# Two graph-attention layers on one core: TensorE's turns two units ahead, the first quad's features ahead of the second's root, and the last three units split in a half and two quarters

## What is computed

```
# first layer: softmax attention under the mask of adj
S = (x @ Wq) @ (x @ Wk).T
P = softmax(S + mask, axis=1)      # mask: lowest float where adj + eye is 0, highest where it is 2
x = layernorm(x + P @ (x @ Wv))
# second layer: additive attention
h = x @ W.T + b
e = leaky((h @ a1)[:, None] + (h @ a2)[None, :] + b_a)
attention = softmax(where(adj > 0, e, -9e15), axis=1)
x = layernorm(x + attention @ h)
```

## Time and profile before

| what | value |
|---|---|
| median of 3 runs | 253.81 us (253.43 to 254.62) |
| profiled execution, its own time | 255.0 us |
| its span, first to last instruction | 253.2 us |
| mean granted TensorE clock | 0.983 |
| PE busy | 236.2 us (93%) |
| DVE busy | 185.3 us (73%) |
| ACT busy | 154.4 us (61%) |
| POOL busy | 61.4 us (24%) |

### The profile page before, as it was taken

One profiled execution on the slowest core, in us unless ns is written; L12 is line 12 of the kernel. 1 busy time (PEld: TensorE's weight loads), 2 busy tenths in 40 slices (PEclk: granted clock), 3 DMA queues, 4 the chain that ended last, 5 costly groups with the idle time before them and its releaser, 6 DMA issues.

```text
span 253.2 us, 4017 instructions
## 1 busy us (share of the span) xinstructions
PE 236.2 (93%) x1523; PEld 133.3 (53%) x1523; DVE 185.3 (73%) x284; ACT 154.4 (61%) x182; POOL 61.4 (24%) x104
## 2 busy tenths in 40 slices
PE   5959999499999999999999999999999999999980
PEld 4947675245555555555555555555555555555450
DVE  1378787967777777779768776977777778797433
ACT  2468978989067999170489994610899982220032
POOL 3284688999200000003030000002300000032122
PEclk9999999679999999999999999999999999999998
DMA  6999999999999999999589999998499920010102
GB/s 187 365 386 389 383 387 383 387 387 386 385 388 383 380 384 387 387 386 385 64 237 305 332 403 392 387 387 298 114 299 339 397 99 3 1 41 3 41 3 88
DMA packets 40939, 71.76 MB, mean 283 GB/s; under 512 B 5843, under 2 KB 6100, under 8 KB 40916
## 3 DMA queue, kind: packets, MB, share of 16 engines
q1 hardware_dynamic: 40480, 71.33, 79.2%
q10 hardware_dynamic: 436, 0.13, 0.2%
HBM read 69.36 MB, written 2.10 MB: 282 GB/s over the span
## 4 chain that ended last, share of the span: by engine, by line
PE 86%; POOL 3%; ACT 3%; DMA 2%; DVE 2%; issue 2%; ACTq 1%; POOLq 0%; DVEq 0%
PE banks L1202 67%; PE banks L1158 10%; PE banks L1217 3%; PE banks L1095 3%; DMA brow<-in_L_gnn_b_W_dram 2%; ACT a L737 2%; PE banks L1110 1%; POOL rstd L597 1%; PE banks L1081 1%; DVE y L1036 0%; POOL f_parts L636 0%; POOL xhat_st L602 0%; POOL frstd L646 0%; POOL feat L629 0%; DVE e_sb L938 0%
## 5 line engine op out<-in xcount | busy, mean ns | idle before, releaser
L1202 PE MATMUL banks<-e_sb,f_parts 128*128 128x512 f16 x768 | 186.1, 391 | 1.5 <-DVE e_sb L938 1.1
L926 DVE SCALAR_TENSOR_TENSOR e_sb<-R,cr_word,banks 128x1024 f32<-128x1024 f32 x124 | 153.8, 1275 | 30.9 <-PE banks L1158 28.3
L737 ACT ACTIVATE a<-a_sb,code_bias 128x2048 fp8e4<-128x2048 int32 x64 | 124.3, 1997 | 2.8 <-DMA a_sb<-in_adj_dram 2.1
L1202 PEld LDWEIGHTS banks<-e_sb,f_parts 128*128 128x128 f16 x768 | 71.6, 97 | 86.8 <-issue 4.0
L646 POOL TENSOR_TENSOR frstd<-frv,minus_half 128x4 f32<-128x4 f32 x8 | 8.1, 1012 | 168.9 <-DVE frv L962 167.6
L1158 PE MATMUL banks<-ident,a 128*128 128x128 f16 x496 | 38.0, 220 | 3.6 <-ACT a L737 3.6
L1158 PEld LDWEIGHTS banks<-ident,a 128*128 128x128 f16 x496 | 32.8, 98 | 15.4 <-ACT a L737 3.9
L728 ACT COPY R<-banks 128x512 f32<-128x512 f32 x8 | 4.7, 587 | 35.9 <-PE banks L1110 35.9
L753 ACT ACTIVATE junk<-y 128x128 f32<-128x128 f32 x28 | 8.3, 298 | 26.8 <-DVE y L953 26.8
L944 DVE RECIPROCAL rden<-banks 128x4 f32<-128x4 f32 x7 | 1.3, 183 | 12.2 <-PE banks L1217 12.2
L1095 PEld LDWEIGHTS banks<-m0c_um,x_tr 128*128 128x128 f32 x64 | 9.6, 224 | 0.8
(11 more groups left out here) (113 smaller groups left out, 101.9 us busy)
## 6 DMA issues: line engine op xcount, KB each, us to landing
a_sb<-in_adj_dram SPq DMA_DIRECT2D x64, 1024.0 KB, 12.4
x_sb<-in_x_dram SPq DMA_DIRECT2D x8, 256.0 KB, 9.9
out_dram<-out_sb SPq DMA_DIRECT2D x8, 256.0 KB, 5.8
w_nat<-in_L_gnn_W_dram ACTq DMA_DIRECT2D x1, 64.0 KB, 3.2
wv<-in_L_gnn_Wv_dram ACTq DMA_DIRECT2D x1, 64.0 KB, 3.1
acol<-in_L_gnn_a_vec_dram SPq DMA_DIRECT2D x1, 1.0 KB, 3.0
bcol<-in_L_gnn_b_W_dram ACTq DMA_DIRECT2D x1, 0.5 KB, 4.5
ba<-in_L_gnn_b_a_dram ACTq DMA_DIRECT2D x1, 0.0 KB
```

The source lines that it names most:

```text
L737: nc.scalar.activation(a8[:, n % 2, Q * h:Q * (h + 1), k * PW:(k + 1) * PW], a_parts[:, m % SLOTS, :, :], ACT.Relu, bias=code_bias[:, :], ...
L926: nc.vector.scalar_tensor_tensor(out=e_sb[:, k % NE, :], in0=R[:, g % 2, :], scalar=cr_word[:, 0, 2 * t + b:2 * t + b + 1], in1=ps_code[s ...
L1202: ins = nc.tensor.matmul(ps_acc[g % 2][h][:, :], f[:, j, :], e_half[:, k % NE, cols, part], start=(j == 0 and n == 0), stop=(j == T - 1 an ...
```

## The change

It has three parts. **Middle:** the turns stay two units ahead, behind the sums, until slot 9 (`LATE = QUADS + 1`) instead of slot 4; slot 9 then makes up the third unit. **Start:** on SP the first piece of `adj` is loaded ahead of the second quad of `x`; on PE `weights(1)` and `layer0(0)` stand ahead of `x_turned(1)`, and four matmuls of `keep_busy` go; on ACT `codes(0)` stands ahead of `copy_xt(1)`; on DVE `words(0)` stands ahead of `divide(1, scores)`; on POOL the first half of quad 0's features stands ahead of `root(1)`. **End:** the second 512 rows of the last three units become two quarters of 256 rows; the last quarter is summed in a bank of its own (`ps_last`) and added by DVE to what earlier units left.

```diff
@@ sizes
-    FIRST = QUADS - 4
+    LATE = QUADS + 1
+    LAST = GW - 2 * P
+        ps_last = ps_row[:, 0:2 * P]
@@ SP
                 load_x(0)
...
+                load(0)
                 load_x(1)
-                load(0)
@@ POOL
                 root(0)
+                features(0, 0)
                 root(1)
-                features(0, 0)
                 features(0, 1)
@@ ACT
                 copy_xt(0)
-                copy_xt(1)
                 act.wait_ge(consts_ready, 12)
                 codes(0)
+                copy_xt(1)
                 exps(0)
                 exps(1)
...
+                act.wait_ge(half_done, 2)
+                nc.scalar.copy(acc_t[:, HW:GW], ps_acc[g % 2][1][:, :]).then_inc(acc_copied, 1)
                 squares(g, 0)
-                act.wait_ge(half_done, 2)
-                for k in range(2):
-                    cols = slice(k * HW // 2, (k + 1) * HW // 2)
-                    nc.scalar.copy(acc_t[:, HW:GW][:, cols], ps_acc[g % 2][1][:, cols]).then_inc(acc_copied, 1)
@@ DVE
                 divide(0, scores)
                 divide(0, inner)
+                words(0)
                 dve.wait_ge(rstd_ready, 2)
                 divide(1, scores)
-                words(0)
                 words(1)
                 half_edges(0, 0, 0)
...
+                    if k == 0:
+                        dve.wait_ge(half_done, 3)
+                        dve.wait_ge(acc_copied, 2 * G)
+                        nc.vector.tensor_tensor(acc_t[:, LAST:GW], ps_last[:, :], acc_t[:, LAST:GW],
+                                                ALU.add).then_inc(acc_copied, 1)
@@ PE, last_sums
-                    for s in units:
-                        for b in range(2):
-                            ins = products(s, b, 1)
-                        if s == S - HALVED:
-                            pe.wait_ge(acc_copied, 2 * G - 1)
-                            pe.wait_ge(y_ready, 2 * G - 2)
-                            projections(0, quad(0), range(Q)).then_inc(fin_mm, 1)
-                    ins.then_inc(half_done, 1)
+                    pe.wait_ge(r_ready, 2 * G)
                     for k in range(2):
-                        pe.wait_ge(acc_copied, 2 * G + k)
-                        projections(1, quad(4), range(2 * k, 2 * k + 2)).then_inc(fin_mm, 1)
+                        for s in units:
+                            if s == S - 1:
+                                if k == 0:
+                                    pe.wait_ge(acc_copied, 2 * G - 1)
+                                    pe.wait_ge(y_ready, 2 * G - 2)
+                                    projections(0, quad(0), range(Q)).then_inc(fin_mm, 1)
+                                else:
+                                    pe.wait_ge(acc_copied, 2 * G)
+                                    projections(1, quad(4), range(2)).then_inc(fin_mm, 1)
+                            for b in range(2):
+                                ins = products(s, b, (slice(HW, LAST), slice(LAST, GW))[k])
+                        ins.then_inc(half_done, 1)
+                    pe.wait_ge(acc_copied, 2 * G + 1)
+                    projections(1, quad(4), range(2, 4)).then_inc(fin_mm, 1)
@@ PE, start
                 weights(0)
+                weights(1)
+                layer0(0)
                 x_turned(1)
-                weights(1)
-                keep_busy(bank[0], 4)
-                layer0(0)
                 layer0(1)
@@ PE, slots
-                    if FIRST < slot < S - NA:
+                    if LATE < slot < S - NA:
                         turn(slot + NA)
                     if slot < S - HALVED:
                         sums(slot)
...
-                    if slot <= FIRST:
+                    if slot <= LATE:
                         turn(slot + 2)
-                    if slot == FIRST:
+                    if slot == LATE:
                         turn(slot + 3)
```

More of the change, by code:

```diff
@@ L1177, in half_sums @@
                         pe.wait_ge(p_half if h == 0 else p_ready, 2 * s + b + 1)
-                        ins = products(s, b, h)
+                        ins = products(s, b, halves[h])
                         if h == 1:
@@ L1193, in sums, with products @@
                         pe.wait_ge(p_ready, 2 * s + b + 1)
-                        products(s, b, 0)
-                        products(s, b, 1).then_inc(mm_done, 1)
-                def products(s, b, h):
+                        products(s, b, halves[0])
+                        products(s, b, halves[1]).then_inc(mm_done, 1)
+                def products(s, b, cols):
                     g, t = divmod(s, U)
                     k, j = 2 * s + b, 2 * t + b
-                    cols = slice(h * HW, (h + 1) * HW)
+                    h, first = divmod(cols.start, HW)
+                    dst, opened = ps_acc[g % 2][h][:, first:first + cols.stop - cols.start], j == 0
+                    if cols.start == LAST:
+                        dst, opened = ps_last[:, :], k == 2 * (S - HALVED)
                     for n, (f, part) in enumerate(((fl, 1), (fh, 1), (fh, 0))):
-                        ins = nc.tensor.matmul(ps_acc[g % 2][h][:, :], f[:, j, :], e_half[:, k % NE, cols, part],
-                                               start=(j == 0 and n == 0), stop=(j == T - 1 and n == 2))
+                        ins = nc.tensor.matmul(dst, f[:, j, :], e_half[:, k % NE, cols, part],
+                                               start=(opened and n == 0), stop=(j == T - 1 and n == 2))
                     return ins
@@ L1212, in project @@
                     projections(q, ps, range(Q)).then_inc(fin_mm, 1)
+                halves = slice(0, HW), slice(HW, GW)
                 def projections(q, ps, rs):
@@ L1226, in last_sums @@
                             pe.wait_ge(p_ready, 2 * s + b + 1)
-                            ins = products(s, b, 0)
+                            ins = products(s, b, slice(0, HW))
                     ins.then_inc(half_done, 1)
-                    for s in units:
-                        for b in range(2):
-                            ins = products(s, b, 1)
-                        if s == S - HALVED:
-                            pe.wait_ge(acc_copied, 2 * G - 1)
-                            pe.wait_ge(y_ready, 2 * G - 2)
-                            projections(0, quad(0), range(Q)).then_inc(fin_mm, 1)
-                    ins.then_inc(half_done, 1)
-                    for k in range(2):
-                        pe.wait_ge(acc_copied, 2 * G + k)
-                        projections(1, quad(4), range(2 * k, 2 * k + 2)).then_inc(fin_mm, 1)
+                    pe.wait_ge(r_ready, 2 * G)
+                    for k in range(2):
+                        for s in units:
[12 more added lines that the diff above has]
+                    projections(1, quad(4), range(2, 4)).then_inc(fin_mm, 1)
                 def keep_busy(ps, n):
```

## The result

The changed kernel takes 255.15 us (median of 20 runs, 254.29 to 256.31), the kernel before on the same chip 254.36 us (20 runs, 253.43 to 255.12). The ratio is 1.0031 [1.0016, 1.0046], so the change costs 0.8 us where I had forecast 0.6 us less. 255.15 lies in the range at its upper end; the sign of the forecast was wrong, and so was the likeliest case. A ratio and its interval are worked out from all runs and can differ by up to 0.2% from the ratio of the two medians; differences in us are those of medians.

The account below looks back on a forecast made before the run. PE, busy 93% of the span, bounds the kernel; only its idle and slow stretches can be won. From the profiled 255.0 us: -6.2 + 2.9 + 2.0 - 0.1 = 253.6; taken as 253.2, range 250.8 to 255.2.

Parts of the forecast that it names:

- the sign of the forecast: Whole kernel: faster, 253.2 us against a median of 253.81 before, within 0.5%.
- the likeliest case: Whole kernel: 252.3 to 254.4 us, middle's gain partly taken back by the start's order and low clock; chance 0.55.
- middle, waiting: Slot 5: PE's 3.57 us idle ahead of `turn(8)`, waiting for ACT's `codes(9)`, goes away.
- middle, clock: Behind slot 5's idle time: slow products and transposes at low clock return to full speed, gaining 0 to 2.6 us.
- start, order: Start: first `half_edges` move from 17.08 to 20.0, 2.9 us later, or 3.7 with `layer0(1)` at the low clock.
- start, clock behind the gap: PE's first products: 3.8 us idle ahead of them brings the low clock, costing 2.0 us (0 to 2.6).
- end: Last `projections` and `y`: last pair of `y` starts 0.1 us sooner, between -0.3 and +0.5; cutting products costs nothing.
- The start's mechanism: Start: `layer0(1)`, `stats(1)`, `divide(0, ...)`, quad 0's features, `root(1)`, `divide(1, scores)`, `half_edges` in turn; PE idles 3.8 us, then low clock.
- `layer0(1)` takes 1.05 at the full clock and 1.75 at the low one: Start, PE: `layer0(1)` starts at 12.2 and ends at 13.3 to 14.0.
- I take the lower value here, 13.35: Start, DVE: `stats(1)` at 13.35 instead of 12.71, 0.65 us later; 1.35 later kept for the range.
- the prediction's 3.7 for the low clock: Start: first `half_edges` 3.7 us later if `layer0(1)` runs at the low clock, instead of 2.9.
- the slower rival: Start: `layer0(1)` at low clock and fall as long as at slot 5, 3.7 + 2.6 = 6.3; 255.0 us; chance 0.13.

Follow-up runs that it names:

- the old stall kept busy: Kernel before with 52 small matmuls on PE in the slot 5 stall, ahead of `turn(8)`: 252.11 us, ratio 0.9925.
- the pair of runs above: Kernel before with the change's middle and `words(0)` ahead, without and with PE's order of the start: 247.94 us and 249.73 us.
- the twelve small matmuls: Middle, `words(0)` ahead and PE's order, plus four small matmuls ahead of `layer0(0)` and eight ahead of `layer0(1)`: 249.41 us, ratio 0.9841.

## Why the prediction was wrong

| term | forecast | measured |
|---|---|---|
| middle, waiting | -3.6 | -3.6 (5.7 - 2.1) |
| middle, clock | -2.6 | -2.1 in medians, -2.6 in the profiled executions |
| start, order | +2.9 | +2.8 in the profiled execution, +4.2 in one with `layer0(1)` at half clock, 4.5 to 4.7 in medians (6.5 or 6.6 for the whole start, less 1.9) |
| start, clock behind the gap | +2.0 | +1.9 in medians, +2.0 in the profiled executions |
| end | -0.1 | +0.2 |

**The terms in the profiled executions.** In each trace I take the time from the first `half_edges` to the start of the last long row of products (the kernel before, with the old stall kept busy, the middle alone, the change; the kernel before starts its `half_edges` at 17.08, the change at 19.90):

```profile
233.08 8.29 PE L1202 MATMUL banks<-e_sb,f_parts 128*128 128x512 f16 x36
...
16.40 1.41 DVE L938 SCALAR_TENSOR_TENSOR e_sb<-R,cr_word,banks 128x512 f32<-128x512 f32 x2 [0.64 <-ACT R L728]
229.83 8.29 PE L1202 MATMUL banks<-e_sb,f_parts 128*128 128x512 f16 x36
...
16.95 1.41 DVE L940 SCALAR_TENSOR_TENSOR e_sb<-R,cr_word,banks 128x512 f32<-128x512 f32 x2 [0.63 <-ACT R L730]
226.78 8.29 PE L1208 MATMUL banks<-e_sb,f_parts 128*128 128x512 f16 x36
...
231.71 8.30 PE L1211 MATMUL banks<-e_sb,f_parts 128*128 128x512 f16 x42
```

It is 216.00 us before, 213.43 with the stall kept busy, 209.83 with the middle alone and 211.81 with the change; in the seven other executions that have the middle and no fall of the clock it is 209.82 to 209.85. So the fall at slot 5 cost 2.57, the waiting 3.60, and the fall at the start 1.98. With 2.82 for the order at the start and 0.03 from the end this makes 2.82 + 1.98 - 6.17 - 0.03 = -1.40, which is what the prediction's terms add up to (253.6 - 255.0). For the two profiled executions the sum was right up to the last store.

**The middle** was right: no wait, a full clock, and DVE's weights in time. Only the clock's share was 0.5 us too large, because I took it from one execution, and that one was slower than the median.

**The start's mechanism** was right, down to each engine of the chain: POOL's `root(1)` behind the features, `divide(1, scores)` behind it, a gap of 3.7 us on PE and half clock behind that. The price of the low clock was right too (2.0 forecast, 1.9 measured). It agrees with the section "HAM oscillation — how this bites in real kernels" of the Trainium skill's page "TensorE: Matmul & The Clock Gate", which I had cited: the 3.57 and 3.71 us of idle time were each followed by half clock, and filling them with matmuls that nobody reads won back 2.1 and 1.9 us.

**The step that failed** is the size of the start's order: "`layer0(1)` takes 1.05 at the full clock and 1.75 at the low one" and "I take the lower value here, 13.35". Two things are wrong in it. First, the choice. Each trace holds a list of the clock's changes, which begins with its first rise. With PE's order of before that rise stands at 11.05 to 12.49 us in all six profiled executions, in the middle of sixteen `layer0` matmuls. With the second eight behind `x_turned(1)` and its copy it stands at 10.85 to 11.35 in three and at 15.83 to 18.05 in four. `layer0(1)` ran at half clock in four of the seven profiled executions that have PE's order of the change: with the start alone, with POOL's order back, with PE kept busy in the gap, and with the middle, `words(0)` and PE's order. The price of PE's order by itself, 1.8 us in the pair of runs above, goes the same way in medians. Why the clock rises late in some executions and not in others stays open: the twelve small matmuls did not settle it. Second, the low value: 1.75 was half of the 3.51 us of the earlier trace rows, which I read as all at low clock, but the clock rose within them; eight at half clock take 2.10. With 2.10 for 1.05, and `layer0(1)` at 12.49 where I had 12.2, the order costs 2.9 + 1.05 + 0.3 = 4.25, which is the 21.25 - 17.08 = 4.2 of the run with PE kept busy. (By its own rows the prediction's 3.7 for the low clock should read 3.6.)

With the measured terms the sum is -5.7 + 4.2 + 1.9 + 0.2 = +0.6 us, against +0.8 measured. The first half of the slower rival, "`layer0(1)` runs at the low clock", was thus the more frequent case in the profiles; its other half, a low clock as costly as at slot 5 (2.6), did not come (1.9). I had given that rival 0.13. The profile of the changed kernel alone would have hidden this, as it shows the other case.

**The base** does not explain the miss. The terms add up to -1.4 us where +0.8 was measured. Setting them against the profiled execution's 255.0, and taking back only a third of its distance from the median of three runs, made the forecast 0.6 under that median. Twenty runs put the kernel before at 254.36, and the same terms from there give 253.0, farther from 255.15 than the 253.2 that I took.

**The start by its moves**, from 255.15 us down: POOL's order with the clock that falls in its gap 4.15, SP's and ACT's order 1.7, PE's order with `words(0)` 0.6, to 248.68 with the start of before. In the pair without the end PE's order came to 1.8, with perhaps some of it given back by `words(0)`. The moves hang together through the clock, so this split holds for this order of undoing them.

**The end**: 0.2 us, within what can be measured from nothing. The prediction's reason holds for the last `y`: the last products end later by about what it saves. Its last pair starts 14.00 to 14.01 us behind the start of the last long row of products in the six profiles with the change's end, and 14.03 to 14.04 in the seven without. The prediction had no term for the last store, which took longer in the profiles with the change's end (see the last section).

The best version here is the change's middle without its start and end, 248.5 us or 2.1% under the kernel before, or the same with `words(0)` ahead.

## What to carry to other kernels

Before a row is split into "so much for each half", ask whether the clock changed inside it; the same form later in the run, or in a second execution, tells. A move that puts one quad first is only as good as the engines that keep both quads in one stream: here DVE and POOL made the first wait for the second, and every move that sent the second quad back delayed both. The gaps of 3.57 and 3.71 us on TensorE in this kernel were paid as waiting and, in most executions, again, some 2 us, as half clock behind them; useless matmuls in the gap won back the second part alone. And a term that hangs on the clock needs more than one profiled execution.

## What was not expected of the hardware

The spread of a kernel's runs tells of the clock. The kernel before varies between 251.37 and 255.21 us over its four groups of runs, the middle alone between 248.43 and 248.78. With the old stall kept busy the runs lie at 251.73 to 252.83, where the fastest runs of the kernel before lie as well. That those are executions in which the clock did not fall is likely: the eight runs at 252.46 us or less have a mean granted clock of 0.993 or 0.994, as the runs with the stall kept busy (0.990 to 0.995), and all others, from 253.22 us on, 0.975 to 0.989. No profile caught one: that of the kernel before shows the fall.

The time of the last store differs. From the start of the last scaling to the end of SP's wait for the store it was 2.8 us with the middle alone (243.40 to 246.18) and 3.8 with the end alone (248.87 to 252.71). Over all profiles it was 3.1 to 3.8 us in the six with the change's end and 2.8 to 3.3 in the seven without. In the profiles of the end alone and of the changed kernel fifteen of its sixteen parts land together, and one about 1 us after them. A fetch of instructions (16 KB) runs close to the store in all these traces, but the traces do not tell which part it meets, and no run took it away: the cause is open.
